# Two-block transformer kernel on one core: pairwise sums, one step late, and the last steps of the fused loop set in a new order

## The reference: what is computed

```python
q_norm_sq = jnp.sum(q * q, axis=-1, keepdims=True)
k_norm_sq = jnp.sum(k * k, axis=-1)[..., None, :]
diff_sq = q_norm_sq + k_norm_sq - 2.0 * jnp.einsum('bhnd,bhmd->bhnm', q, k)
denom = jnp.maximum((1.0 - q_norm_sq) * (1.0 - k_norm_sq), 1e-06)
cosh_arg = jnp.maximum(1.0 + 2.0 * diff_sq / denom, 1.0)
attn = softmax(-arccosh(cosh_arg))          # 16 heads, 256 x 256 each
x = x + (attn @ v) @ wo.T                   # first residual
x = x + relu(layernorm(x) @ w1 + b1) @ w2 + b2
```

## Time and profile before

| | |
|---|---|
| median of 3 runs | 2449.32 us (2448.59 to 2451.76) |
| profiled execution, its own time | 2456.33 us |
| span in its trace | 2454.2 us, mean granted PE clock 0.907 |
| start of the fused loop's stage | about 1320 us into the span |
| body of a batch in the loop | 33.3 us |
| share of 1500 to 2300 us busy | PE 620.66, DVE 747.53, ACT 769.50, POOL 760.66 of 800 us |

### The profile page before, as it was taken

How to read it: one execution, slowest core, us unless ns; L and a number is a source line. 1 busy time by engine, 2 the same in 40 slices (tenths; PEclk the granted TensorE clock), 3 DMA queues, 4 the chain that set the end, 5 groups by cost and what they waited for, 6 DMA issues and landing times. The chain is left out here.

```text
span 2454.2 us, 50808 instructions
## 1 busy us (share of the span) xinstructions
PE 2089.9 (85%) x15438; PEld 1566.8 (64%) x15438; DVE 1956.8 (80%) x5939; ACT 1767.4 (72%) x3085; POOL 1627.2 (66%) x1866
## 2 busy tenths in 40 slices
PE   4999999999999996999997677777777778777876
PEld 4677777777777775888885445555555555555554
DVE  4677776776777774778775899999999999999992
ACT  2666666666666762444432799999999999999996
POOL 2776676766666750000001899999999999999993
PEclk7999999999999996999997579888888988889888
DMA  5000000000000003353450466776666777666674
GB/s 142 1 2 2 2 1 2 2 1 2 1 2 1 2 2 70 86 119 76 96 114 10 93 127 130 139 138 128 124 119 127 141 141 134 119 129 124 129 142 80
DMA packets 81388, 184.24 MB, mean 75 GB/s; under 512 B 9479, under 2 KB 31530, under 8 KB 81195
## 3 DMA queue, kind: packets, MB, share of 16 engines
q0 software_dynamic: 36864, 134.23, 29.1%
q1 hardware_dynamic: 36010, 43.38, 7.9%
q10 hardware_dynamic: 8320, 4.19, 0.7%
HBM read 42.85 MB, written 4.72 MB: 19 GB/s over the span
## 5 line engine op out<-in xcount | busy, mean ns | idle before, releaser
L1557 POOL TENSOR_TENSOR spare<-spare,u 128x1024 f32<-128x1024 f32 x192 | 456.2, 2376 | 16.0
L542 ACT ACTIVATE prob<-s_ps,nmax 128x128 f32<-128x128 f32 (+1 forms) x1024 | 364.4, 432 | 132.2 <-DVE nmax L599 132.2
L599 DVE CUSTOM_DVE_ANT_0 s_ps<-s_ps,mask 128x128 f32<-128x128 f32 (+1 forms) x1024 | 340.7, 385 | 100.7 <-issue 76.4
L1633 DVE TENSOR_SCALAR u<-d_ps 128x1024 f32<-128x1024 f32 x256 | 312.1, 1219 | 48.7 <-PE i_ps L1374 48.1
L579 POOL TENSOR_TENSOR g_lo<-g_all,g_hi 128x512 fp32r<-128x512 f32 x256 | 329.1, 1286 | 21.4
L1637 DVE SCALAR_TENSOR_TENSOR u<-i_ps,u 128x1024 f32<-128x1024 f32 x256 | 313.5, 1225 | 13.2 <-DVE u L1633 0.5
L1374 PE MATMUL d_ps<-rowsT 28*128 28x256 f32 x1024 | 144.7, 357 | 149.5 <-DVE u L1637 145.9
L534 ACT COPY g_all<-g_ps 128x512 f32<-128x512 f32 x256 | 151.5, 592 | 162.6 <-PE g_ps L63 161.5
L1514 ACT ACTIVATE u<-u 128x1024 f32<-128x1024 f32 x256 | 257.0, 1056 | 1.7 <-DMA u<-spare 1.6
L1517 ACT ACTIVATE u<-u 128x1024 f32<-128x1024 f32 x256 | 255.7, 1051 | 0.0
L1374 PEld LDWEIGHTS d_ps<-rowsT 28*128 28x128 f32 x1024 | 92.4, 208 | 246.3 <-issue 241.7
(11 more groups left out here) (275 smaller groups left out, 5795.2 us busy)
## 6 DMA issues: line engine op xcount, KB each, us to landing
u<-spare POOLq DMA_DIRECT2D x256, 512.0 KB, 12.2
w_all<-w_rows SPq DMA_DIRECT2D x128, 256.0 KB, 5.9
x<-L_attn_x ACTq DMA_DIRECT2D x8, 512.0 KB, 13.9
y<-x SPq DMA_DIRECT2D x32, 128.0 KB, 10.0
wkqv<-L_attn_Wkqv SPq DMA_DIRECT2D x4, 528.0 KB, 8.9
gate_rows<-L_ffn_gate_proj SPq DMA_DIRECT2D x1, 512.0 KB, 14.4
up_rows<-L_ffn_up_proj SPq DMA_DIRECT2D x1, 512.0 KB, 11.1
down_cols<-L_ffn_down_proj SPq DMA_DIRECT2D x1, 512.0 KB, 13.0
```

Source lines behind the costliest of these rows:

```text
L542: last = nc.scalar.activation(prob[:, kind, at, :].rearrange("p c n -> p (c n)"), s_ps[kind][:, at.start * P:at.stop * P], ACT.Exp, bias=n ...
L599: last = nc.vector.tensor_tensor_reduce(out=scores, in0=scores, in1=keep.mask[:, N - width:N], scale=-1.0, scalar=3.4e38, op0=ALU.add, op1 ...
L1557: nc.gpsimd.tensor_tensor(extra, extra, pair, ALU.mult).then_inc(prod_done, 1)
L1633: nc.vector.tensor_scalar(u[:, slot(i, p), :], d_ps[:, :], 0.0, None, ALU.max).then_inc(dist_done, 1)
```

## The change

- The sums go two pairs at a time: four accumulating DMAs of 128 x 2048 floats in place of eight of 128 x 1024. Three are issued behind the sixth product, the fourth (pairs 6 and 7) behind the first product of the next batch.
- POOL adds 2 to all 1024 columns in one instruction.
- The tokens of batch b+2, and those of the MLP of batch b-3, are turned at the end of body b, and into `o_ps`; before, this stood behind the first pairs product of body b+1, and went into `misc`.
- DVE makes the next batch's features behind ratio 5 instead of ratio 4; in the program's table `FEATURES_AT = 5` counts from 0, so it is the sixth ratio.
- PE turns row tiles 0, 1 at p = 6 and 2, 3, 4 at p = 7 (before: 0 at 5, 1 and 2 at 6, 3 and 4 at 7).
- The second half of the ReLU on ACT moves between the logarithms and the exponentials of pairs 4 and 5; `dve_y` moves from p = 1 to p = 2; one keep-busy call at p = 7 is gone; some waits move with their work.

```diff
-    SUMS_BEHIND = {5: (0, 1, 2, 3, 4, 5, 6, 7)}
+    SUMS_BEHIND = {5: (0, 2, 4)}
-    BUSY_AHEAD, BUSY_BEHIND = {5: 1}, {4: 4, 7: 1}
+    FEATURES_AT = 5
+    BUSY_AHEAD, BUSY_BEHIND = {5: 1}, {4: 4}
...
         def pe_turn_x(pe, b):
             pe.wait_ge(xh_done, (b + 1) * TB)
-            after(pe, res_done, b - 3)
-            after(pe, hi_done, b * TB)
-            after(pe, qkv_taken, b * TB)
+            after(pe, xT_done, b)
...
         def pool_sum(pool, b, p, i):
-            pool.wait_ge(root_done, b * HP + p + 1)
-            nc.gpsimd.dma_start(u[:, slot(i, p), :], spare[:, p, :], accum_op=ALU.add).then_inc(sum_landed[p], 16)
+            pool.wait_ge(root_done, b * HP + p + 2)
+            at = slot(i, p)
+            nc.gpsimd.dma_start(u[:, at:at + 2, :], spare[:, p:p + 2, :], accum_op=ALU.add).then_inc(sum_landed[p // 2], 16)
...
-            nc.gpsimd.tensor_tensor(extra[:, 0:4], pair[:, 0:4], twos[:, :], ALU.add)
-            nc.gpsimd.tensor_scalar(extra[:, 4:2 * W2], pair[:, 4:2 * W2], 1.0, 2.0, ALU.mult, ALU.add).then_inc(raised, 1)
+            nc.gpsimd.tensor_scalar(extra, pair, 1.0, 2.0, ALU.mult, ALU.add).then_inc(raised, 1)
...
@@ PE @@
                 pe_fold_w1(pe)
+                pe.wait_ge(w1_folded, 1)
+                pe_turn_x(pe, 1)
...
-                        if one_after and p == 0:
-                            pe_turn_x(pe, b + 1)
-                        if four_before and p == 0:
-                            if not one_after:
-                                pe.wait_ge(res_done, b - 2)
-                            pe_turn_x4(pe, b - 4, (i - 4) % TURN, misc, N)
...
-                            for r in {5: (0,), 6: (1,), 7: (3,)}.get(p, ()):
+                            for r in {6: (0,), 7: (2, 3)}.get(p, ()):
                                 pe_turn_rows(pe, b + 1, r)
...
-                            for r in {6: (2,), 7: (4,)}.get(p, ()):
+                            for r in {6: (1,), 7: (4,)}.get(p, ()):
                                 pe_turn_rows(pe, b + 1, r)
+                        if p == HP - 1 and one_after:
+                            if one_before:
+                                pe.wait_ge(o_copied, 2 * b)
+                            if two_after:
+                                pe_turn_x(pe, b + 2)
+                            if three_before:
+                                pe_turn_x4(pe, b - 3, i, o_ps, N)
                         if one_before:
-                            if p == HP - 1:
-                                pe.wait_ge(o_copied, 2 * b)
                             pe_keep_busy(BUSY_BEHIND.get(p, 0))
+                        if p == 0 and one_after:
+                            pe.wait_ge(xT_done, b + 2)
...
@@ ACT @@
+                def weights(b, i, p, relu_of=None):
+                    for n in range(2):
+                        act_weights(act, b, p + n, i, True)
+                    if relu_of is not None:
+                        act_relu(act, relu_of, 1)
+                    for n in range(2):
+                        act_weights(act, b, p + n, i, False)
...
@@ POOL @@
                         pool_product(pool, b, p, i)
+                        if p == 0 and one_before:
+                            pool_sum(pool, b - 1, HP - 2, (i - 1) % TURN)
...
@@ DVE @@
-                        if p == 1 and five_before:
+                        if p == 2 and five_before:
                             dve_y(dve, b - 5)
...
-                            if p == 4:
+                            if p == FEATURES_AT:
                                 after(dve, relu_done, 2 * (b - 3))
                                 dve_features(dve, b + 1)
```

More of the change, by code:

```diff
@@ L1311, in hyperbolic_attention_and_mlp @@
         prod_done, root_done, ln_done, w_done, pv_done = S_("prod_done"), S_("root_done"), S_("ln_done"), S_("w_done"), S_("pv_done3")
-        sum_landed = [S_(f"sum_landed{n}") for n in range(HP)]
+        sum_landed = [S_(f"sum_landed{n}") for n in range(HP // 2)]
         o_copied, o_turned, rec_done, attn_done = S_("o_copied3"), S_("o_turned3"), S_("rec_done3"), S_("attn_done3")
@@ L1322, in wait_sum @@
         def wait_sum(engine, b, p):
-            after(engine, sum_landed[p], 16 * (b + 1))
+            after(engine, sum_landed[p // 2], 16 * (b + 1))
         def slot(i, p):
@@ L1338, in pe_turn_x @@
             pe.wait_ge(xh_done, (b + 1) * TB)
-            after(pe, res_done, b - 3)
-            after(pe, hi_done, b * TB)
-            after(pe, qkv_taken, b * TB)
+            after(pe, xT_done, b)
             for j in range(TB):
-                last = nc.tensor.transpose(misc[:, j * P:(j + 1) * P], xh[:, j, :], keep.ident)
+                last = nc.tensor.transpose(o_ps[:, j * P:(j + 1) * P], xh[:, j, :], keep.ident)
             last.then_inc(xh_turned, 1)
@@ L1347, in pe_qkv @@
             pe.wait_ge(xT_done, b + 1)
+            if j == 0:
+                after(pe, res_done, b - 3)
             after(pe, hi_done, b * TB + j)
@@ L1435, in pe_hidden @@
         def pe_hidden(pe, b, half, rows_read):
-            if half == 0:
-                pe.wait_ge(w1_folded, 1)
             pe.wait_ge(rowsT_done[half], rows_read)
@@ L1467, in act_xT @@
             after(act, qkv_ready, b * TB)
-            nc.scalar.copy(xTs[:, 0, :], misc[:, 0:N]).then_inc(xT_done, 1)
+            nc.scalar.copy(xTs[:, 0, :], o_ps[:, 0:N]).then_inc(xT_done, 1)
         def act_both_xT(act, b, b4):
@@ L1474, in act_both_xT @@
             after(act, h_ready, 2 * b4)
[L1475 removed]
+            nc.scalar.copy(xTs[:, :, :].rearrange("p s n -> p (s n)"), o_ps[:, :]).then_inc(xT_done, 1)
         def act_hi(act, b, j):
@@ L1814, in _ @@
                 act_fold_w1(act)
-                def weights(b, i, p):
-                    for logarithm in (True, False):
-                        for n in range(2):
-                            act_weights(act, b, p + n, i, logarithm)
+                def weights(b, i, p, relu_of=None):
[5 more added lines that the diff above has]
+                        act_weights(act, b, p + n, i, False)
                 def body(b, i, one_before, two_before, three_before, four_before, five_before, one_after, two_after):
@@ L1837, in body @@
                         if four_before and p == 2:
-                            for half in range(2):
-                                act_relu(act, b - 4, half)
+                            act_relu(act, b - 4, 0)
                     if three_before:
@@ L1892, in body @@
                             pool_sum(pool, b, n, i)
-                            if n == NORM4_BEHIND and three_before:
-                                pool_norm4(pool, b - 3, i)
+                        if p == NORM4_BEHIND and three_before:
+                            pool_norm4(pool, b - 3, i)
                 written_out(body)
+                pool_sum(pool, END, HP - 2, END % TURN)
                 for b in (END - 2, END - 1, END):
                     pool_norm4(pool, b, b % TURN)
-                for p in range(HP):
+                for p in range(0, HP, 2):
                     wait_sum(pool, END, p)
```

13 lines of the change are left out of this document (5 added, 8 removed).

## The result

The changed kernel takes 2463.51 us (median of 6 runs, 2458.55 to 2466.92) against 2449.52 for the kernel before on the same chip (6 runs, 2448.59 to 2451.76). The ratio is 1.0056, 95% interval [1.0045, 1.0067]. Slower by 14 us was forecast as slower by 11. How much of that is a right answer for the right reasons is what the experiments were for.

The account below looks back on a forecast made before the run. The DVE-PE loop was taken to set the pace: a body of 33.65 instead of 33.33 us gives +9.6 over 30 bodies, plus 1.4 at the start, +11, so the median 2449.3 becomes 2460 us; range 2440 to 2482.

Parts of the forecast that it names:

- the stop of 0.40: DVE stop behind ratio 3, where only the statistics stand; 0.40 us a body, said to come with any clock.
- What bounds the loop: Last stage: DVE and PE wait on each other through ratio, pairs product and distances; body 33.33 us, DVE work 31.78.
- POOL worth 0: Fewer issues and merged adds leave POOL 27 to 32 us a body; worth 0, since POOL already waits 1.0 for DVE.
- The stop at row tile 2: DVE's copy of row tile 2 behind ratio 7 waits for PE: about 0.9 us at full clock, 1.55 at low.
- The 0.82 behind ratio 0 mostly goes: DVE's stop of 0.82 us behind ratio 0, seen after longer low-clock stretches, mostly disappears; 0.1 kept.
- Features behind ratio 5: Features fill DVE's gap ahead of the distances of pair 6, so its 0.30 stop goes; gain 0.3 to 0.4 us.
- `dve_y` behind the third product: Moving `dve_y` to p = 2 takes away its stop on DVE, 0.26 us a body.
- Tokens: Token transposes on PE replace a keep-busy product of about the same length; no cost was put on them.
- The clock: PE at low clock in six to eight of ten bodies; average body 33.5 to 33.7 us, 33.65 taken.
- low clock in every body: Rival: longer idling ahead of ratio 7 lowers PE's clock every time; body 33.8 to 34.1, 2466 to 2474 us; chance 0.25.
- The start: Ahead of the first body PE waits for the copy of `w1` and turns tokens; +1.4 us, bounds 0 and 2.
- The transfers: Sums stay hidden; a pair lands in 7.6 us, limit 8.3; at 10.5 the body would be 42 us, chance 0.03.

Follow-up runs that it names:

- e1: The changed kernel with row tile 2 turned at p = 6, ahead of the pairs product that waits for ratio 7; 2447.57 us, ratio 1.0009.
- e10: The kernel before with late features, ReLU's second half moved, row tile 0 at p = 6, 1 and 2 behind it, ahead of the pairs product; 2418.04 us, ratio 0.9875.
- e12: The changed kernel with tokens turned into misc at the body's start again and the keep-busy product behind the last product back; 2472.29 us, ratio 1.0103.
- e11: The kernel before with only the four pairwise sums of 1024 KB and the merged addition; 2444.99 us, ratio 0.9995.
- e3: The changed kernel with features behind ratio 4, row tiles and ReLU's second half at their old places; 2474.57 us, ratio 1.0122.
- e7: e3 with `dve_y` also back behind the second product, as in the kernel before; 2476.43 us, ratio 1.0110.
- e5: The kernel before with one edit, row tile 2 turned behind the pairs product at p = 7; 2482.36 us, ratio 1.0129.
- e2: The changed kernel with eight sums of 512 KB, all behind the sixth product; 2464.73 us, ratio 1.0077.
- e4: The changed kernel with three more keep-busy products at p = 5, where PE waits for ratio 6; 2460.31 us, ratio 1.0054.
- e6: e1 with PE's y product and its wait for ACT's copy at p = 1 instead of p = 0; 2463.74 us, ratio 1.0052.
- e9: e6 with `dve_y` at p = 3 instead of 2; 2572.78 us, ratio 1.0529.

## Why the prediction was right, and where it was not

e1, e10, e12 and the changed kernel make a square. e10 lacks the sums and the place of y, which e11 and e3 against e7 price at nothing, but with the features in their old place; that they are worth nothing behind the late features as well is taken over from there. Ratios to the kernel before:

| | row tile 2 ahead of the pairs product | behind it |
|---|---|---|
| tokens at the body's start | e10 0.9875 | e12 1.0103 |
| tokens at the end of the body before | e1 1.0009 | changed 1.0056 |

Read along one way from the kernel before: the features edit -1.25%, row tile 2 behind the pairs product +2.3%, the tokens -0.5%, together the +0.56% that was measured. Read along the other: the features edit -1.25%, the tokens +1.3%, row tile 2 +0.5%. Row tile 2 and the tokens each cost much where they come first, and little or nothing where they come second. The waits say why. I summed DVE's waits between 1500 and 2300 us by the place where they stand and divided by the bodies (us in a body):

| DVE waits ahead of | before | e5 | e10 | e12 | e1 | changed |
|---|---|---|---|---|---|---|
| copy of row tile 2 | 0 | 1.36 | 0 | 1.48 | 0 | 1.36 |
| distances 1 | 0.35 | 0.06 | 0 | 0.05 | 0 | 0.02 |
| distances 2 | 0 | 0 | 0 | 0.28 | 1.29 | 0.05 |
| distances 4 | 0.4 | 0.4 | 0.4 | 0.4 | 0.4 | 0.4 |
| distances 6 | 0.53 | 0.42 | 0.17 | 0 | 0 | 0 |
| `dve_y` | 0.26 | 0.05 | 0 | 0 | 0 | 0 |
| together | 1.54 | 2.26 | 0.59 | 2.19 | 1.68 | 1.82 |

Row tile 2's stop stands ahead of the one that the tokens bring (distances 2), and where both edits are made it hides it: 1.29 us become 0.05.

The last column is my sum for the body, term by term: work 31.78, the stop of 0.40, 0.9 to 1.55 for row tile 2, and up to 0.1 for the rest. Measured: 33.50 - 1.82 = 31.68, 0.4, 1.36 and 0.07. As an account of the changed kernel it holds. As prices of its parts it does not, and that it came out so near has luck in it: the tokens, which I put at nothing, are at nothing only behind row tile 2's stop.

- *What bounds the loop.* Right. The DVE-PE loop sets the pace, and POOL's and ACT's waits are worth nothing while it does. e11 and the 5.7 us that POOL now waits show it for POOL, e10 for ACT: once most of DVE's stops are gone (0.59 us are left), the body falls to 32.14 and stays at ACT's work.
- *POOL worth 0.* Right. An issue of 1024 KB costs no more than one of 512: 0.87 us in the median of the trace after, against 0.86 in e2 and 1.18 in the kernel before. The merged addition takes 1.04 us, and 1.32 behind an issue. POOL is busy 650.03/24 = 27.1 us a body, the lower end of the 27 to 32.
- *The stop at row tile 2.* Right in place and size. Predicted 0.9 at the full clock and 1.55 at the low one, measured 0.77 and 1.52 (a few bodies 0.1 less), one in each body.
- *Its cover.* "The 0.82 behind ratio 0 mostly goes" came true: the stop ahead of distances 1 fell from 0.35 us a body to 0.02, and e5 shows that row tile 2 alone does this (0.06). For row tile 2 my numbers make 33.65 - 31.78 - 0.40 - 0.59 = 0.9 us (0.59 being the part of the old 33.33 that is neither work nor the stops of 0.40, 0.30 and 0.26), 27 us in 30 bodies; e5 measured 33. What I did not see is that the cover is not row tile 2's alone. The late features take the same stops away (e10), so behind them row tile 2 has nothing left to cover, and its price is 54 us (e12 against e10). The clock goes with it there: the projection is slow in 1 body of e10 and in all 24 of e12, where the stop is the long one in 23 of 24.
- *Features behind ratio 5.* The mechanism was right, the term was mis-sized: "Gain 0.3 to 0.4 us" for a stop that goes. Measured with e10: 33.33 to 32.14, 1.2 us in a body of the profiled executions, and 27 us between the medians, 0.9 in a body. The stop ahead of distances 6, which I had read off one body as 0.30, was 0.53 in the mean and lost 0.36. I priced that one stop and left out that those ahead of distances 1 (0.35) and of `dve_y` (0.26) go as well, though `dve_y` stays where it was in e10. The low clock, at which I had read the 0.82, is gone there too: 1 projection of 24 is slow, where it was 16.
- *`dve_y` behind the third product.* Its stop went, and the gain of 0.26 did not come, at least not with the features in their old place: 1.0122 with it and 1.0110 without (e3, e7). With the late features the stop is gone without the move (e10).
- *Tokens.* Wrong step: "The token transposes replace a keep-busy product of about the same length." That priced PE's work, not the bank. A wait for ACT's copy came into PE's queue ahead of the y product, with a pairs product behind it. It costs 28 us (e7 against e11), and 1.3%, 33 us, in e1 against e10, where it is a stop of 1.29 us ahead of distances 2. Beside the late tile 2 it is covered, and the earlier turning gains 11 us (changed against e12).
- *The clock.* I took the low clock in six to eight bodies of ten. At the pairs product behind ratio 7 and at the stop it is 19 of 24, 7.9 of ten. At the projection behind them 4 more are nearly low, so the rival "low clock in every body" came close in its cause, but not in its price: 33.50 us, not 33.8. The Trainium skill, "TensorE: Matmul & The Clock Gate" (Why this matters for your kernels), advises against idle gaps between bursts of matmuls; the gaps that it names are longer than those of 0.4 to 2.6 us at this place. Stretched to such gaps, its rule would have the change lose and e4 win. The rows agree for the first, and for e10 against e12. For e4 they show that the granted clock can rise from 0.87 to 0.92 without a gain that can be told (1.0054 against 1.0056).
- *The start.* Predicted +1.4, measured -0.6; the end, predicted 0, +1.6.
- *The transfers.* Right that they are hidden: ACT never waits for one in the list of after. The condition was wrong. The quickest pair lands in 7.0 us (predicted 7.6), but the median is 10.2, more than the 8.3 that I had called the limit and close to the 10.5 at which I had put the body at 42 us. Four times 10.2 us is more than the body of 33.50, so the times to landing overlap, and they are not what a transfer adds.

What stays open is why the profiled body of the changed kernel grew by only 0.17 us, 5 us over 30 bodies, when the medians differ by 14. Single executions of the kernel before differ by 7 us, and one profile of each cannot tell how these spread over the bodies. Nor was the stop of 0.40 ahead of distances 4 tried, which every version has.

## What to carry to other kernels

When two engines hand a buffer back and forth, the place of a small step ahead of or behind the handover is worth more than the work saved on the engines beside it: here 11, 33 or 54 us, by what stands around it, against next to nothing for a seventh of GpSimd's work. Price such a move twice, once for the stop that it makes, and once for the idle time that it opens on the other engine. Ask also which stops it hides, since the next edit may have hidden them already: prices measured alone do not add up. When a change has several parts, try each alone and beside the others before the sum is believed: one part of this change, taken by itself, was 1.25% faster, and its companions took all of it back and more. And when an output goes to another bank, list who holds that bank and what is queued behind the wait, as both misses here (e6, e9) and the cost of the tokens came from that.

## What the runs showed of the hardware

- PE falls to 1.2 GHz behind short waits when they follow one another. In the changed kernel it waits 1.20 to 1.83 us ahead of the pairs product behind ratio 6, and that product is slow (0.58 instead of 0.38 us) in 9 of 24 bodies; it then waits again, 0.41 to 2.11 us, and the next pairs product is slow in 19 of 24. In e10 the first of these waits is 0.55 to 1.18 us in 17 of 25 bodies, and the row tiles behind it are all at 2.4 GHz. In the other 8 it is 1.65 or 1.76 us, and the clock falls; after three row tiles turned without a long break it is back at 2.4 GHz by the projection in 7 of the 8. In the changed kernel, with two row tiles there and a second wait, the projection is at the full clock in none of 24.
- An accumulating transfer of 1024 KB costs POOL the same issue as one of 512 KB (0.87 us in the median, against 0.86 in e2). The quickest lands in 7.0 us against 4.7 for 512 KB, less than twice; the medians (10.2 us for 1024 KB, 11.7 in e11; 12.2 for 512 KB, 11.1 in e2) are those of transfers in a queue and do not tell what one costs. The same 134.23 MB took 27.1% of the span of 16 DMA engines in the large pieces and 29.1% in the small ones. The Trainium skill, "DMA: Bandwidth & Descriptors" (SDMA does more than copy), states a largest element count of 2048 for such sums; the rows of a pair have just 2048, and no row here shows a cost at that length.
